# Three parts of a tuned transformer kernel: paired rounds of the value product, one plain weight slice instead of two, output weights prepared earlier

## The chip, the core and the metric

The kernel runs on one core of a Trainium2 chip as a single launch. The metric is the device time of one execution in microseconds. A core has five engines that run their own instruction streams and wait for each other with semaphores: TensorE (PE, matrix products and transposes), VectorE (DVE), ScalarE (ACT), GpSimd (POOL) and SyncE (SP, which issues DMAs). Weight loads of TensorE are shown as an engine of their own, PEld.

## The reference, cut to what matters

1024 tokens of width 512 pass six layers in float32. Two of them are a mixture of experts, one is a causal attention; these are the ones that the change touches.

```
x = x + 0.5 * ffn(layernorm(x))            # mixture of experts ("moe")
x = x + attn(layernorm(x))                 # causal attention ("causal")
x = x + 0.5 * ffn(layernorm(x))            # the same mixture of experts
x = x + 0.5 * butterfly(...); x = x + full_attention(...); x = x + 0.5 * butterfly(...)

# ffn: 16 experts, each token goes to 4 of them, and one shared expert
scores = sigmoid(x @ gate_w.T) + bias;  topk_w, topk_idx = top_k(scores, 4)
out = sum over chosen e of cw[e] * (silu(x @ Wg[e].T) * (x @ Wu[e].T)) @ Wd[e].T

# attn: 32 query heads of 16, 8 key/value heads, rotary embedding, causal mask
scores = einsum('bqhd,bkhd->bhqk', q, k) / 16
probs = softmax(where(mask, scores, min))
ctx = einsum('bhqk,bkhd->bqhd', probs, v)
out = ctx @ w_dense.T + b_dense
```

## The kernel before, in words

Each layer is one or more blocks; in a block every engine has its own list of instructions, and all engines meet at its end. Semaphore counts set the order between the engines, the written order sets it on an engine: an instruction that waits holds everything behind it on its engine.

**Split products.** A float32 product is made in one of two ways. "Plain" feeds float32 operands to TensorE (two recorded matmuls for each product). "Split" cuts both operands into a high part in the float32r type (`hi`, a cast on ScalarE) and the rest (`lo`, a subtraction on VectorE), and sums three products: hi with hi, hi with lo, lo with hi (`product`, L191).

**Routed blocks** (`routed_blocks`, L730 to L838). Tokens are sorted by expert into 47 blocks of 128 token slots, in each of the two mixture layers. For block b the engines do this:

- GpSimd gathers the rows of block b+3 (L708) and scatters the results of block b-3 with an add (L715).
- TensorE makes the gate and up product of block b: four slices of 128 inputs, of which the first `PLAIN` = 2 are plain (L730) and the other `SPLIT` = 2 split (L735). Then it transposes the rows of block b+2 (L744) and the hidden values of block b-1 (L751), and makes the down product of block b-2, split (L191).
- ScalarE casts the gate/up weights of block b+1 (L778, 1024 elements a partition), the down weights of block b+1 (L783), copies the output of block b-3 (L790), applies silu to block b (L795), casts the transposed rows of b+2 (L801) and the hidden values of b-1 (L806).
- VectorE makes the low parts of both weights (L819, L822), z = silu times up times routing weight (L828), a copy of the plain part of the transposed rows (L833), the low part of the split slices (L834), and the low part of the hidden values (L838).

ScalarE and VectorE read two table entries (expert and weight offset) into registers at the start of each step; w_hi and w_lo have two buffers each.

**Causal layer, core block** (L1469 on). The work goes in 8 groups of 4 query heads. A group has 12 steps u: u = 0 to 3 are query half 0 with key blocks 0 to 3; u = 4 to 11 are query half 1, where u = 4, 6, 8, 10 take key blocks 0 to 3 and u = 5, 7, 9, 11 key blocks 4 to 7. The steps on the diagonal are 0 to 3 and 5, 7, 9, 11. Step u has for each of 4 heads h a score product on TensorE (L1652, 128 to 512 columns), and an exponential on ScalarE (L1746) into the probability buffer `prob`. On a diagonal step GpSimd then zeroes a triangle of it (L1592, "mask"). When the step is complete, a round of values follows: V(u) is 4 plain products (one head each, 8 recorded matmuls) with `v_now`, each on 32 of the array's columns (L1669). TensorE issues V(u-1) in step u behind the third head. There are two `prob` buffers, so the exponentials of step u wait for V(u-2).

In between TensorE makes, for the next group, 48 products for row maxima (L1631, and L1634 on the diagonal), four in each step, which VectorE reduces (L1782); three PSUM banks hold the scores and three the maxima. GpSimd splits the maxima (L1558 to L1572; first half after mask 3, second half ahead of the next group), TensorE transposes them (L1642), ScalarE copies them after the exponentials of step 6 (L1731), and GpSimd then issues three small DMAs with them (`put_maxima`, L1578). On GpSimd's list this stands behind mask 5 and ahead of mask 7. In the last group nothing is made for a next one.

**Causal layer, dense block** (L1845 on). After the core block SP loads the output weights and the bias, ScalarE casts the weights to their high part (L1874, behind the casts of two tiles), GpSimd makes the low part (L1851) and adds the bias to all of x (L1853). TensorE transposes the 8 tiles of the context (L170), then makes 8 products of 12 matmuls (L191). VectorE makes the low parts (L182), waits for the bias, and adds each product to x (L1885), followed by its statistics (L86).

## Time and profile before

| | |
|---|---|
| time, median of 3 runs | 1372.45 us (1371.72 to 1373.23) |
| the profiled execution, its own time | 1367.37 us |
| its span, first to last instruction | 1365.6 us |
| PE busy | 1144.0 us (84%) |
| PEld busy | 723.2 us (53%) |
| DVE busy | 837.1 us (61%) |
| ACT busy | 665.5 us (49%) |
| POOL busy | 537.6 us (39%) |

The stages in order of time: mixture of experts to about 340 us (its 47 routed blocks from 85 us), causal layer from there to 766 us (its core block from 430 to 724 us, its dense block from 725 us), second mixture to about 1110 us, then butterfly, full attention and butterfly. Busy shares are averages over these stages. Instructions of register loads and semaphores are not counted as busy, so a gap whose cause is given as "issue" can be such work of the engine's own instruction reader.

### The profile page before, as it was taken

Reading aid. Unit: us, or ns where it says so; the run is one execution under the profiler, and the core shown is the slowest. Engines: PE = TensorE matmul, PEld = TensorE weight load, DVE = VectorE, ACT = ScalarE, POOL = GpSimd, SP = SyncE. Lnnn points to the kernel's source line nnn. Section 1 sums busy time; section 2 is a strip of 40 time slices with the busy share of each in tenths; the row PEclk is TensorE's granted clock in tenths of the full one; section 3 lists DMA queues with packets and bytes.
Section 4 is the critical chain, followed back from the end, with each engine's and each line's share of the span. In section 5 each row is a group of like instructions: output and inputs, shape, how many; then the busy total and the mean of one; then the engine's idle time right before and its main releaser. Section 6 shows DMA issues by size and latency. Waiting matters only on the chain. (4 is left out here: it accounts for less than half of the span.)

```text
span 1365.6 us, 22222 instructions
## 1 busy us (share of the span) xinstructions
PE 1144.0 (84%) x5800; PEld 723.2 (53%) x5801; DVE 837.1 (61%) x1527; ACT 665.5 (49%) x1218; POOL 537.6 (39%) x578
## 2 busy tenths in 40 slices
PE   5979999996284899999985796999999808777687
PEld 4747677674173344444424584676776605465454
DVE  4857777773455787777722565777777524445542
ACT  3136666663232277777772222666666503334133
POOL 4325555553673233333324324455555442050130
PEclk9979999998587699999998797999999957979879
DMA  9256989555405440000001454689955550010001
GB/s 349 100 203 156 241 238 248 100 104 90 183 35 133 95 89 2 1 1 1 1 1 39 181 189 170 179 206 264 253 107 100 81 167 0 4 37 0 20 12 62
DMA packets 63497, 151.64 MB, mean 111 GB/s; under 512 B 12560, under 2 KB 17488, under 8 KB 58832
## 3 DMA queue, kind: packets, MB, share of 16 engines
q1 hardware_dynamic: 40224, 99.83, 21.4%
q0 software_dynamic: 22592, 50.27, 19.4%
q10 hardware_dynamic: 624, 0.85, 0.4%
q8 instruction: 27, 0.44, 0.1%
q14 instruction: 30, 0.25, 0.1%
HBM read 105.75 MB, written 44.97 MB: 110 GB/s over the span
## 5 line engine op out<-in xcount | busy, mean ns | idle before, releaser
L715 POOL DMA_INDIRECT moe_acc_rows<-moe_out_rows,moe_token_of x94 | 165.4, 1760 | 196.5 <-ACT moe_out_rows L790 190.4
L1782 DVE TENSOR_REDUCE causal_top<-causal_mx 128x1 f32<-128x512 f32 (+3 forms) x384 | 192.0, 550 | 58.6 <-PE causal_mx L1634 50.5
L1746 ACT ACTIVATE causal_prob<-causal_sc 128x512 f32<-128x512 f32 (+3 forms) x384 | 169.9, 492 | 73.2 <-PE causal_sc L1652 70.7
L819 DVE TENSOR_TENSOR moe_w_lo<-moe_raw,moe_w_hi 128x1024 fp32r<-128x1024 f32 x94 | 115.1, 1225 | 112.7 <-ACT moe_w_hi L778 99.6
L730 PE MATMUL moe_gu<-moe_raw,moe_xt_plain 128*128 x376 | 180.5, 603 | 2.4 <-ACT moe_w_hi L778 2.4
L1631 PE MATMUL causal_mx<-causal_ks,causal_qs 96*128 (+4 forms) x384 | 130.9, 351 | 19.2 <-DMA causal_qs<-causal_parts 15.7
L778 ACT CAST moe_w_hi<-moe_raw 128x1024 fp32r x94 | 98.2, 1045 | 95.2 <-issue 90.8
L1652 PE MATMUL causal_sc<-causal_qs,causal_ks 99*128 (+3 forms) x384 | 123.7, 333 | 2.3 <-ACT causal_prob L1746 1.7
L708 POOL DMA_INDIRECT moe_rows<-moe_xn_rows,moe_token_of x94 | 93.3, 992 | 75.2 <-DVE moe_z L828 31.8
L822 DVE TENSOR_TENSOR moe_down_lo<-moe_raw,moe_down_hi 128x1024 fp32r<-128x1024 f32 x94 | 114.5, 1218 | 0.0
L735 PE MATMUL moe_gu<-moe_w_hi,xt_hi 128*128 128x512 f32 x188 | 112.7, 600 | 0.0
L730 PEld LDWEIGHTS moe_gu<-moe_raw,moe_xt_plain 128*128 128x128 f32 x376 | 71.6, 192 | 57.1 <-issue 49.4
L783 ACT CAST moe_down_hi<-moe_raw 128x1024 fp32r x94 | 98.1, 1043 | 0.0
L1592 POOL TENSOR_SCALAR_AFFINE_SELECT causal_prob<-causal_prob 128x512 f32<-128x512 f32 x64 | 40.9, 640 | 136.9 <-ACT causal_prob L1746 136.8
L1669 PE MATMUL causal_po<-causal_prob,causal_v_now 128*32 128x512 f32 (+3 forms) x768 | 81.8, 498 | 5.4 <-POOL causal_prob L1592 4.5
L1652 PEld LDWEIGHTS causal_sc<-causal_qs,causal_ks 99*128 (+1 forms) x384 | 36.8, 98 | 86.0 <-ACT causal_prob L1746 35.2
L191 PE MATMUL moe_y<-moe_down_hi,moe_zt_hi 128*128 128x512 f32 x188 | 81.9, 436 | 0.0
L735 PE MATMUL moe_gu<-moe_w_hi,xt_lo 128*128 128x512 f32 x188 | 74.5, 396 | 0.0
L191 PE MATMUL moe_y<-moe_down_hi,moe_zt_lo 128*128 128x512 f32 x188 | 74.2, 395 | 0.0
L735 PE MATMUL moe_gu<-moe_w_lo,xt_hi 128*128 128x512 f32 x188 | 74.1, 394 | 0.0
L191 PE MATMUL moe_y<-moe_down_lo,moe_zt_hi 128*128 128x512 f32 x188 | 73.9, 393 | 0.0
L145 POOL TENSOR_SCALAR var_eps<-mean_var 128x1 f32<-128x1 f32 x48 | 13.3, 276 | 147.6 <-DVE mean_var L98 147.4
(273 smaller groups left out, 2425.0 us busy)
## 6 DMA issues: line engine op xcount, KB each, us to landing
moe_raw<-in_w_gu SPq DMA_DIRECT2D x34, 1024.0 KB
moe_raw<-in_w_down SPq DMA_DIRECT2D x34, 512.0 KB
causal_qs<-causal_parts SPq DMA_DIRECT2D x42, 128.0 KB, 3.3
moe_acc_rows<-moe_zeros SPq DMA_DIRECT2D x2, 2304.0 KB, 15.2
moe_acc_rows<-x SPq DMA_DIRECT2D x18, 256.0 KB, 2.0
moe_xn_rows<-xn SPq DMA_DIRECT2D x2, 2048.0 KB, 10.9
x<-moe_acc_rows SPq DMA_DIRECT2D x16, 256.0 KB, 5.3
xn<-moe_acc_rows SPq DMA_DIRECT2D x16, 256.0 KB, 5.9
```

The lines of the kernel that those rows point to most:

```text
L191: last = nc.tensor.matmul(out, a, b, start=(n == 0), stop=(n == 3 * len(pairs) - 1))
L715: pool.indirect_dma_start(acc_rows[a], bass.IndirectOffsetOnAxis(ap=token_of[:, b - 3:b - 2].bitcast(U32), axis=0), out_rows[(b - 3) % OUT ...
L730: nc.tensor.matmul(gu[s][:, :], xt_plain[s][:, k, :], raw[:, bass.ds(at + k * 2 * FI, 2 * FI)], start=(k == 0), stop=False)
L735: last = nc.tensor.matmul(gu[s][:, :], xt(half, s, k), part[s][:, k - PLAIN, :], start=False, stop=(k == KT - 1 and half is m.xt_lo))
L778: nc.scalar.copy(w_hi[1 - s][:, :, :], raw[:, bass.ds(at + SPLIT_AT, GU_COLS - SPLIT_AT)].rearrange("p (k n) -> p k n", k=SPLIT)).then_inc ...
L783: nc.scalar.copy(down_hi[(c + 1) % 4][:, :, :], raw[:, bass.ds(at + GU_COLS, W_COLS - GU_COLS)].rearrange("p (i h) -> p i h", i=IT)).then_ ...
L819: nc.vector.tensor_tensor(w_lo[1 - s][:, :, :], raw[:, bass.ds(at + SPLIT_AT, GU_COLS - SPLIT_AT)].rearrange("p (k n) -> p k n", k=SPLIT), ...
L822: nc.vector.tensor_tensor(down_lo[(c + 1) % 4][:, :, :], raw[:, bass.ds(at + GU_COLS, W_COLS - GU_COLS)].rearrange("p (i h) -> p i h", i=I ...
L1631: last = nc.tensor.matmul(mx[i % BANKS][:, 0:w], qs[0:STACK, bass.ds(at, P)], ks[0:STACK, bass.ds(gn * S + kc * CH, w)], start=True, stop= ...
L1652: nc.tensor.matmul(sc[b][:, o:CH], ks[0:STACK + MROWS, bass.ds(g * S + kb * P, P)], qs[0:STACK + MROWS, bass.ds(g * QG + (h * S + c * CH + ...
L1746: nc.scalar.activation(prob[u % 2][:, h, o:CH], sc[(u * QPK + h) % BANKS][:, o:CH], ACT.Exp, scale=SCALE).then_inc(exp_done, 1)
L1782: nc.vector.tensor_reduce(top[:, kc, t, h:h + 1], mx[i % BANKS][:, 0:w], AX.X, ALU.max).then_inc(mx_read, 1)
```

## The change

`PLAIN` becomes 1, so three of four gate/up slices are split; the buffers of the output rows move into `m.xn`. In the core block the rounds of values are issued in pairs, V(u-2) and V(u-1) behind the third head of each even step u, and `prob` has three buffers, so that the exponentials of step u wait for V(u-3). The output weights are loaded in the core block in two halves; GpSimd casts, subtracts and adds the bias there, one slice and one tile a group, in `prepare_dense`, which stands in step 6 behind `put_maxima`. The dense block keeps the transposes, the products and the additions, with the transposes of the next tile ahead of each product, and VectorE finishing tile t-2 behind the low part of tile t.

```diff
--- before.py
+++ after.py
@@ -34,7 +34,7 @@
 EARLY = 3
-PLAIN = 2
+PLAIN = 1
 SPLIT = KT - PLAIN
@@ -625,7 +625,7 @@
         rows = [sb(f"rows{s}", [P, ROW]) for s in range(RING)]
-        out_rows = [sb(f"out_rows{s}", [P, H]) for s in range(OUTS)]
+        out_rows = [m.xn[:, s, :] for s in range(OUTS)]
         xt_plain = [sb(f"xt_plain{s}", [P, PLAIN, P]) for s in range(2)]
@@ -1273,6 +1273,7 @@
         ks = outer.enter_context(nc.sbuf_tensor(f"{name}_ks", [P, KV * S], BF16))
+        dense_in, wd_half, wd_ready, x_biased = sem("dense_in"), sem("wd_half"), sem("wd_ready"), sem("x_biased")
@@ -1478,6 +1479,8 @@
+            wd_hi = outer.enter_context(nc.sbuf_tensor(f"{name}_wd_hi", [P, KT, H], F32R))
+            wd_lo = outer.enter_context(nc.sbuf_tensor(f"{name}_wd_lo", [P, KT, H], F32R))
             BANKS = 3
@@ -1486,6 +1489,8 @@
             ident = sb("ident", [P, P], BF16)
+            wd_raw = sb("wd_raw", [P, KT // 2, H])
+            b_out = sb("b_out", [P, H])
             warm = sb("warm", [1, 1])
@@ -1493,7 +1498,8 @@
             neg_turned = [sb(f"neg_turned{h}", [MROWS * QPK, CH], BF16) for h in range(NCH)]
-            prob = [sb(f"prob{s}", [P, QPK, CH]) for s in range(2)]
+            PROBS = 3
+            prob = [sb(f"prob{s}", [P, QPK, CH]) for s in range(PROBS)]
             out_t = sb("out_t", [P, CH])
@@ -1539,9 +1545,13 @@
                         sp.dma_start(ks[a * HD:(a + 1) * HD, 0:S], parts_dram[K_PART[a], 0:HD, :]).then_inc(stack_in, 16)
+                    sp.dma_start(wd_raw[:, :, :], m.dram["w_dense"][:, 0:KT // 2, :]).then_inc(dense_in, 16)
+                    sp.dma_start(b_out[:, :], m.dram["b_dense"].rearrange("(a h) -> a h", a=1).broadcast_to([P, H])).then_inc(dense_in, 16)
                     with sp.Fori(1, KV) as g:
...
                         load(g)
+                    sp.wait_ge(wd_ready, KT // 2)
+                    sp.dma_start(wd_raw[:, :, :], m.dram["w_dense"][:, KT // 2:KT, :]).then_inc(dense_in, 16)
@@ -1589,8 +1599,22 @@
                         pool.wait_ge(exp_done, g * (NS * QPK) + ((u + 1) * QPK + BANKS))
-                        nc.gpsimd.affine_select(prob[u % 2][:, :, o:o + P], prob[u % 2][:, :, o:o + P], [[0, QPK], [1, P]],
+                        nc.gpsimd.affine_select(prob[u % PROBS][:, :, o:o + P], prob[u % PROBS][:, :, o:o + P], [[0, QPK], [1, P]],
                                                 ALU.is_ge, 0.0, base=0, channel_multiplier=-1).then_inc(masked, 1)
+                    def prepare_dense(g):
+                        if g == 0:
+                            pool.wait_ge(dense_in, 32)
+                        if g == KT // 2:
+                            pool.wait_ge(dense_in, 48)
+                        if g < KT:
+                            raw = wd_raw[:, g % (KT // 2), :]
+                            nc.gpsimd.tensor_copy(wd_hi[:, g, :], raw).then_inc(wd_half, 1)
+                            pool.wait_ge(wd_half, g + 1)
+                            nc.gpsimd.tensor_tensor(wd_lo[:, g, :], raw, wd_hi[:, g, :].bitcast(F32),
+                                                    ALU.subtract).then_inc(wd_ready, 1)
+                        nc.gpsimd.tensor_tensor(m.x[:, g, :], m.x[:, g, :], b_out[:, :], ALU.add).then_inc(x_biased, 1)
@@ -1605,6 +1629,8 @@
                                 put_maxima(g + 1, 0)
+                            if u == C0 + 2:
+                                prepare_dense(g)
@@ -1667,7 +1693,7 @@
                             last = nc.tensor.matmul(po[2 * HD * h:2 * HD * (h + 1), o:CH], v_now[:, kb, :],
-                                                    prob[u % 2][:, h, o:CH], start=(kb == 0), stop=(kb == (c + 1) * TC - 1))
+                                                    prob[u % PROBS][:, h, o:CH], start=(kb == 0), stop=(kb == (c + 1) * TC - 1))
                         last.then_inc(pv_done, 1)
@@ -1685,9 +1711,11 @@
                                     maximum(g + 1, UPS * u + h)
-                                if h == 2 and u >= 1:
+                                if h == 2 and u % 2 == 0 and u >= 2:
+                                    values(g, u - 2)
                                     values(g, u - 1)
-                                elif h == 2 and not first:
+                                elif h == 2 and u == 0 and not first:
+                                    values(g - 1, NS - 2)
                                     values(g - 1, NS - 1)
@@ -1718,6 +1746,7 @@
                     group(KV - 1, False, False)
+                    values(KV - 1, NS - 2)
                     values(KV - 1, NS - 1)
@@ -1739,11 +1768,11 @@
                             o = max(0, kb * P - c * CH)
-                            if some(g * NS + u):
-                                act.wait_ge(pv_done, g * NS + u)
+                            if some(g * NS + u - 1):
+                                act.wait_ge(pv_done, g * NS + u - 1)
                             for h in range(QPK):
                                 act.wait_ge(sc_done, g * (NS * QPK) + (u * QPK + h + 1))
-                                nc.scalar.activation(prob[u % 2][:, h, o:CH], sc[(u * QPK + h) % BANKS][:, o:CH], ACT.Exp,
+                                nc.scalar.activation(prob[u % PROBS][:, h, o:CH], sc[(u * QPK + h) % BANKS][:, o:CH], ACT.Exp,
                                                      scale=SCALE).then_inc(exp_done, 1)
@@ -1829,62 +1858,45 @@
-            wd_raw = sb("wd_raw", [P, KT, H])
-            wd_hi = sb("wd_hi", [P, KT, H], F32R)
-            wd_lo = sb("wd_lo", [P, KT, H], F32R)
-            b_out = sb("b_out", [P, H])
             xp = [pb(f"xpd{s}", [P, CH]) for s in range(2)]
...
             cm = NormSems(sem, "ctx")
-            wd_in, wd_half, wd_ready, x_biased, y_done, x_done = (
-                sem("wd_in"), sem("wd_half"), sem("wd_ready"), sem("x_biased"), sem("y_done"), sem("x_done"))
+            y_done, x_done = sem("y_done"), sem("x_done")
             with nc.Block() as block:
-                @block.sync
-                def _(sp):
-                    sp.dma_start(wd_raw[:, :, :], m.dram["w_dense"]).then_inc(wd_in, 16)
-                    sp.dma_start(b_out[:, :], m.dram["b_dense"].rearrange("(a h) -> a h", a=1).broadcast_to([P, H])).then_inc(wd_in, 16)
-                @block.gpsimd
-                def _(pool):
-                    pool.wait_ge(wd_half, 1)
-                    nc.gpsimd.tensor_tensor(wd_lo[:, :, :], wd_raw[:, :, :], wd_hi[:, :, :].bitcast(F32),
-                                            ALU.subtract).then_inc(wd_ready, 1)
-                    nc.gpsimd.tensor_tensor(m.x[:, :, :], m.x[:, :, :], b_out[:, :].unsqueeze(1).broadcast_to([P, T, H]),
-                                            ALU.add).then_inc(x_biased, 1)
                 @block.tensor
                 def _(pe):
-                    for t in range(T):
-                        transpose_tile(m, pe, cm, xp[t % 2], t, ready=False)
-                    pe.wait_ge(wd_ready, 1)
-                    for t in range(T):
-                        pe.wait_ge(cm.xt_lo, t + 1)
-                        if t >= 2:
-                            pe.wait_ge(x_done, t - 1)
-                        rows = slice(t * P, (t + 1) * P)
-                        product(nc, yp[t % 2][:, :], [(m.xt_hi[:, k, rows], m.xt_lo[:, k, rows], wd_hi[:, k, :], wd_lo[:, k, :])
-                                                      for k in range(KT)]).then_inc(y_done, 1)
+                    pe.wait_ge(wd_ready, KT)
+                    for t in range(T + 1):
+                        if t < T:
+                            transpose_tile(m, pe, cm, xp[t % 2], t, ready=False)
+                        if t >= 1:
+                            pe.wait_ge(cm.xt_lo, t)
+                            if t >= 3:
+                                pe.wait_ge(x_done, t - 2)
+                            rows = slice((t - 1) * P, t * P)
+                            product(nc, yp[(t - 1) % 2][:, :], [(m.xt_hi[:, k, rows], m.xt_lo[:, k, rows], wd_hi[:, k, :],
+                                                                 wd_lo[:, k, :]) for k in range(KT)]).then_inc(y_done, 1)
...
                 def _(act):
-                    for t in range(2):
-                        hi_tile(m, act, cm, xp[t % 2], t)
-                    act.wait_ge(wd_in, 32)
-                    nc.scalar.copy(wd_hi[:, :, :], wd_raw[:, :, :]).then_inc(wd_half, 1)
-                    for t in range(2, T):
+                    for t in range(T):
                         hi_tile(m, act, cm, xp[t % 2], t)
...
                 def _(dve):
-                    for t in range(T):
-                        lo_tile(m, dve, cm, xp[t % 2], t)
-                    dve.wait_ge(x_biased, 1)
-                    for t in range(T):
+                    def finish(t):
                         dve.wait_ge(y_done, t + 1)
...
+                    dve.wait_ge(x_biased, T)
+                    for t in range(T):
+                        lo_tile(m, dve, cm, xp[t % 2], t)
+                        if t >= 2:
+                            finish(t - 2)
+                    finish(T - 2)
+                    finish(T - 1)
```

## Rows read from the trace of the kernel before

**Rows 1.** Busy time by stretch: stretch, length, busy (instructions) by engine, clock, DMA share, GB/s.

```profile
480.00:720.00 240.00, 230.37 (x1723) 92.89 (x1715) 168.49 (x351) 170.40 (x390) 76.71 (x173) 1.00 0.06 13
```

**Rows 2.** Timeline, TensorE, one routed block: start us, us, engine, line, operation, count.

```profile
203.96 1.88 PE L730 MATMUL moe_gu<-moe_raw,moe_xt_plain 128*128 x4
...
205.91 0.40 PE L735 MATMUL moe_gu<-moe_w_lo,xt_hi 128*128 128x512 f32 x1
...
207.07 0.60 PE L744 MATMUL moe_tx<-ident,moe_rows 128*128 128x128 f32 x4
...
209.12 1.88 PE L730 MATMUL moe_gu<-moe_raw,moe_xt_plain 128*128 x4
```

**Rows 3.** Groups by line and form: count | busy us, mean ns | idle before, releaser.

```profile
L819 DVE TENSOR_TENSOR moe_w_lo<-moe_raw,moe_w_hi 128x1024 fp32r<-128x1024 f32 x94 | 115.1, 1225 | 112.7 <-ACT moe_w_hi L778 99.6 <-issue 13.0
...
L778 ACT CAST moe_w_hi<-moe_raw 128x1024 fp32r x94 | 98.2, 1045 | 95.2 <-issue 90.8 <-SPq L676 4.5
```

**Rows 4.** Timeline, routed blocks, ScalarE: hidden values, weights of the next, silu.

```profile
202.81 0.38 ACT L806 CAST moe_zt_hi<-moe_tz 128x256 fp32r<-128x256 f32 x1
...
204.19 1.05 ACT L778 CAST moe_w_hi<-moe_raw 128x1024 fp32r x1 [1.00 <-issue]
...
207.27 0.39 ACT L795 ACTIVATE moe_silu<-moe_gu 128x256 f32<-128x256 f32 x1 [0.61 <-PE moe_gu L735]
```

**Rows 5.** Timeline, routed blocks, VectorE: an early step, and the end of a later one.

```profile
98.42 1.22 DVE L819 TENSOR_TENSOR moe_w_lo<-moe_raw,moe_w_hi 128x1024 fp32r<-128x1024 f32 x1
...
102.18 1.23 DVE L819 TENSOR_TENSOR moe_w_lo<-moe_raw,moe_w_hi 128x1024 fp32r<-128x1024 f32 x1
...
224.30 0.41 DVE L838 TENSOR_TENSOR moe_zt_lo<-moe_tz,moe_zt_hi 128x256 fp32r<-128x256 f32 x1
225.99 1.23 DVE L819 TENSOR_TENSOR moe_w_lo<-moe_raw,moe_w_hi 128x1024 fp32r<-128x1024 f32 x1 [1.27 <-issue]
```

**Rows 6.** Timeline, core block, GpSimd: the same instruction in two groups that follow.

```profile
597.16 0.40 POOL L1584 COPY causal_v_now<-causal_v_all 128x256 f32<-128x256 f32 x1
...
629.51 0.40 POOL L1584 COPY causal_v_now<-causal_v_all 128x256 f32<-128x256 f32 x1
```

**Rows 7.** Timeline, core block, TensorE: a wait, and a round of values with its neighbours.

```profile
607.14 0.23 PE L1631 MATMUL causal_mx<-causal_ks,causal_qs 96*128 x1 [0.20 <-DVE causal_top L1782]
...
608.33 0.38 PE L1631 MATMUL causal_mx<-causal_ks,causal_qs 96*128 x1
608.63 1.07 PE L1669 MATMUL causal_po<-causal_prob,causal_v_now 128*32 128x512 f32 x8
609.63 0.39 PE L1652 MATMUL causal_sc<-causal_qs,causal_ks 99*128 x1
```

**Rows 8.** Timeline, core block: end of step 6 on ScalarE, then GpSimd's put and mask 7.

```profile
613.17 0.60 ACT L1746 ACTIVATE causal_prob<-causal_sc 128x512 f32<-128x512 f32 x1 [0.79 <-PE causal_sc L1652]
...
614.52 1.62 POOL L1578 DMA_DIRECT2D causal_qs<-causal_neg_turned  x3 [3.15 <-ACT causal_neg_turned L1731]
616.38 0.64 POOL L1592 TENSOR_SCALAR_AFFINE_SELECT causal_prob<-causal_prob 128x512 f32<-128x512 f32 x1 [0.23 <-ACT causal_prob L1746]
```

**Rows 9.** Groups by line and form on GpSimd, columns as in rows 3.

```profile
L133 POOL TENSOR_TENSOR x<-x,xn 128x512 f32<-128x512 f32 x16 | 20.1, 1259 | 23.2 <-POOLq L620 23.2
...
L914 POOL CAST butter_perm_row<-butter_perm_row_i 128x512 f32<-128x512 int32 x2 | 1.7, 843 | 0.0
L1099 POOL TENSOR_TENSOR full_wo_lo<-full_wo_raw,full_wo_hi 128x512 fp32r<-128x512 f32 x1 | 1.4, 1443 | 0.0
```

**Rows 10.** Timeline, dense block: first transposes, first addition, last matmul.

```profile
725.35 1.94 PE L170 MATMUL causal_xpd<-ident,xn 128*128 128x128 f32 x8 [1.93 <-PEq L1527]
...
747.02 0.69 DVE L1885 TENSOR_TENSOR x<-causal_yp,x 128x512 f32<-128x512 f32 x1 [6.48 <-POOL x L1853]
...
764.44 0.40 PE L191 MATMUL causal_yp<-causal_wd_hi,xt_lo 128*128 128x512 f32 x1
```

**Rows 11.** Start of the core block: the stretch of its first loads, columns as in rows 1.

```profile
432.00:434.00 2.00, 0.00 (x0) 0.00 (x0) 0.08 (x1) 0.95 (x1) 0.00 (x0) 0.50 1.11 147
```

4 lines of the change are left out of this document (2 added, 2 removed).

## The prediction, made before the changed kernel was run

> **What bounds the kernel now.** I read the page's busy shares first (TensorE 84%, the next engine 61%), then the busy time by stretch, then the timelines of one routed block, one group of the core block and the dense block, because an average over six stages prices nothing. The reader is to see three things. In the core block TensorE is busy 230.37 of 240 us [rows 1]. In a routed block it has no gap at all: one block follows the other after 209.12 - 203.96 = 5.16 us [rows 2], and 94 blocks make 485 us of the span. In the dense block the order is set by preparation: the first addition waits for GpSimd's bias until 747.02, while TensorE had started at 725.35 [rows 10]. So TensorE's time counts in two stages, and waiting in the third.
>
> **One plain slice instead of two.** The matmuls of one kind follow each other at (207.07 - 205.91) / 5 = 0.232 us, so the first split one ran at 205.68 and two plain slices took 205.68 - 203.96 = 1.72 us, 0.86 each [rows 2]. A split slice is three matmuls, 0.70 us. Each block saves 0.16 us of TensorE, 94 blocks 15.0 us, and the period becomes 5.00.
>
> What pays is elsewhere. The weight cast grows from 1024 to 1536 elements: at most in proportion, 0.52 us on 1.045 (ScalarE) and 0.61 us on 1.225 (VectorE) [rows 3]; the cast of the transposed rows grows by half as well, some 0.13 us at the same rate, and VectorE's copy loses what its subtraction gains. ScalarE has 0.61 us to spare before silu [rows 4], and needs up to 0.65 more in a period 0.16 shorter. It is short by up to 0.20 on this count. Against that stands its gap of 1.00 us marked "issue" ahead of the weight cast [rows 4]: the register loads of a step stand behind the cast of the hidden values, which waits for TensorE. An engine that is late finds that wait already met and loads while it still computes; VectorE did so in the early step, 98.42 to 102.18, 3.76 us with no gap [rows 5]. I take it that ScalarE does the same and hides the shortage. VectorE needs 3.76 + 0.61 = 4.37 us of 5.00. The first block of each layer has nothing to hide the longer cast and subtraction: +0.5 us twice. Sum -14.0; bounds -15.0 and, if ScalarE hides nothing, (5.20 - 5.16) x 94 = +3.8.
>
> **Rounds of values in pairs.** A round of 512 columns starts 0.30 us after the last matmul ahead of it, of which 0.23 is that matmul's own stream, and the next score product starts 1.00 us later [rows 7]: 1.07 us, where the same columns cost 0.86 in a plain slice. So a round pays 0.21 us to get in and out, and a pair pays once, if its second round runs into the first. The Trainium skill, "TensorEngine Tiling (Array Packing)", section Key Properties, says that changing the tiling mode drains TensorE while tiles within a mode work independently. By that rule the whole 0.21 is saved in each pair, 10.1 us; the trace shows a cost of that form, but no two rounds side by side. The other bound is the 0.07 ahead of a round alone, 3.4 us. I take 0.20 x 48 pairs = 9.6 us, nearer to the rule's form because the four products of a round already overlap.
>
> TensorE also idles 9.6 us in 240 [rows 1], with a period of 629.51 - 597.16 = 32.35 us [rows 6] some 1.3 us a group; part are waits for VectorE's reductions [rows 7] and for masks. V(u-2) now stands ahead of V(u-1) and covers the mask's 0.64. On the other side the three PSUM banks run empty in a pair of 1.9 us, and ScalarE and VectorE restart from nothing after it. Between all idle gone (-1.3 x 7 = -9) and 0.25 us lost at each pair (+10) I take -4.5, the masks' part. Pairing: -14.1, bounds -19 and +7.
>
> **The dense preparation on GpSimd.** It stands behind `put_maxima` and ahead of mask 7, and that mask is what V(7) waits for; behind V(7) stand the fourth score of step 8 and all that follows on TensorE. The put starts at 614.52 and takes 1.62, to 616.14 [rows 8]. The prepared slice costs a cast of 0.84, a subtraction of 1.44 and the bias of 1.26 [rows 9], 3.54 us, then two hand-overs of 0.1 and the mask 0.64: mask 7 is done at about 620.5. TensorE wants it sooner. The step's last exponential ended at 616.38 - 0.23 = 616.15 [rows 8] with V(6) ahead of it on TensorE; V(6) now moves behind three more scores, ScalarE's own rate lets the exponential come some 0.45 earlier (615.7), V(6) then starts near 616.3 and V(7) could at 617.2. The stall is 3.3 us in groups 0 to 3. In groups 4 to 6 only the bias is added: 616.14 + 1.26 + 0.64 + 0.1 = 618.15, a stall of 0.95. Group 7 has no put. Sum 4 x 3.3 + 3 x 0.95 = +16.1; bounds +19 (both tensor operations at 1.44 and the cast at 1.26) and +8 (the pair comes 2 us later, because ScalarE restarts late). Before, this work lay behind the core block; nothing hides it here but GpSimd's idle time, and the place in its list is what takes that away.
>
> **The dense block.** It ended at 764.44 + 0.23 = 764.67 [rows 10]. Now weights and bias are ready. Two tiles are transposed in 1.94 us at the lower clock, 725.35 to 727.3; with the wait for the first low part the first product starts at 727.9 and, at twice 0.232 a matmul as long as the clock is low, ends at 733.5. Seven products of 12 x 0.232 = 2.79 and six transposed tiles of about 0.5 (four transposes recorded 0.60, rows 2) give 22.5: end 756.0, -8.7 us. Bounds -5 (the low clock lasts a product longer) and -10.5 (it rises at once).
>
> **Loads at the start of the core block.** 0.5 MB of weights and 0.25 MB of bias now stand on SP's queue behind the first key loads and beside the first query loads on ScalarE's. The DMA engines are full there, 1.11, at 147 GB/s [rows 11], so 0.77 MB cost 5.2 us if all ahead of the queries, nothing if all behind. I take half, +2.5. The second half of the weights waits on SP behind all group loads, where nobody needs SP. The output rows in `m.xn` add no instruction: 0.
>
> **Sum.** -14.0 - 14.1 + 16.1 - 8.7 + 2.5 = -18.2 us. The profiled execution took 1367.37 us around a span of 1365.6; it becomes 1349.2. The median of the runs is 5.1 us above it, and the same step from there gives 1372.45 - 18.2 = 1354 us.
>
> **Rivals.**
> 1. The mask is not late. For it: GpSimd is busy only 76.71 of 240 us [rows 1], and a pair may start later than I reckon. Against: the order of its list, and 3.5 us do not fit between the put and the mask. Then 1354 - 16 = 1338 us.
> 2. ScalarE bounds the routed blocks. For it: the shortage of up to 0.20 us. Against: its register loads can overlap once it is late. With growth in proportion the period is 5.20 and the time 1354 + 18 = 1372; with 0.1 less, 1362.
> 3. The pairs starve the other engines and pairing gives nothing: 1354 + 14 = 1368 us. For it: the three banks; against: VectorE waits for TensorE as often as the reverse.
> 4. The other side: VectorE's register loads don't overlap in the looped part. There they lie bare, 224.30 to 225.99, 1.69 us from the start of the last subtraction to the next weight subtraction, marked "issue" [rows 5]. If so its step is 3.76 + 0.61 + 1.69 - 0.41 = 5.65 us. It decides as soon as a step passes 5.16: 94 x (5.65 - 5.00) = +61, 1415 us. Against: the early steps made the same loads within 3.76 us, and the later gap stands where VectorE had time.
>
> **How the numbers follow.** The forecast 0.60, rival 1 0.12, rival 2 0.16, rival 3 0.05, rival 4 0.07. The forecast's own range is 1346 to 1362. The range of 1342 to 1368 takes in the bounds of the single terms and most of rival 2, and leaves out rivals 1 and 4 and a remainder, some 0.2. About 0.2%, 2.7 us, is what a measurement of this kernel can tell from no change. Faster by more: the forecast, rival 1, most of rivals 2 and 3, 0.87; within it 0.05, from rivals 2 and 3; slower 0.08, rival 4 and the worst of rival 2.
>
> **What would show it.** Right: routed blocks 5.00 us apart with no gap on TensorE; 8 + 8 value matmuls in 1.9 us; V(7) waiting for mask 7 some 3 us in groups 0 to 3, 1 us in groups 4 to 6; the dense block's last product near 31 us after its first transpose; the first maximum product of the core block 2 to 3 us later. Wrong: gaps on TensorE in the routed blocks ending with the weight subtraction; mask 7 ready before V(6) ends; a second round that costs 1.07 again; a group period of the core block far from 34 us in groups 0 to 3 and 31.5 us in groups 4 to 6.

## The result, and the profile after

The changed kernel takes 1380.51 us (median of 6 runs, 1375.74 to 1385.47), the kernel before 1370.59 beside it (6 runs): ratio 1.0074, 95% interval 1.0052 to 1.0096, so 7 to 13 us slower. Ratios below are against runs of the kernel before that were taken beside each kernel. The prediction said 1354. The profiled execution took 1379.36 us around a span of 1377.6.

The stages, each from its first instruction on TensorE to the first (or last) of the next, us:

```
stage                                               before   after  difference
start to the first routed block, layer 1             86.10   84.79   -1.3
routed blocks, layer 1                              243.86  242.35   -1.5
first transpose of the attention layer to scores    107.11  108.67   +1.6
core block, first score to last transpose           257.29  278.95  +21.7
dense block, first transpose to last product         39.49   30.15   -9.3
routed blocks, layer 2                              244.87  244.33   -0.5
all other                                           386.88  388.36   +1.5
```

These are one profiled execution each. The loss is in the core block, and the routed blocks give 2 us where 14 were forecast. The third stage holds the new loads: it takes 108.1 to 108.7 us in the four traces with them, and 105.8 to 107.1 in the eight traces of kernels that are as before up to there.

TensorE's share of busy time hardly moves, and would not tell where to look. This is the page's line, and then the stretch that [rows 1] shows of before: busy 218.33 of 240 us where it was 230.37.

```profile
PE 1136.6 (83%) x5894; PEld 743.7 (54%) x5895; DVE 879.0 (64%) x1527; ACT 708.5 (51%) x1217; POOL 589.4 (43%) x592
```

```profile
480.00:720.00 240.00, 218.33 (x1595) 93.11 (x1597) 164.83 (x345) 151.85 (x351) 88.67 (x181) 0.98 0.06 15
```

**Routed blocks.** An undisturbed block is as predicted: 208.63 - 203.64 = 4.99 us on TensorE (before 5.16, [rows 2]). But some blocks are not undisturbed. The second row below has TensorE waiting 1.05 us at the row transposes for the gather:

```profile
203.64 1.02 PE L730 MATMUL moe_gu<-moe_raw,moe_xt_plain 128*128 x2
...
208.63 1.02 PE L730 MATMUL moe_gu<-moe_raw,moe_xt_plain 128*128 x2
...
218.01 0.66 PE L744 MATMUL moe_tx<-ident,moe_rows 128*128 128x128 f32 x4 [1.05 <-DMA moe_rows<-moe_xn_rows,moe_token_of]
```

Such waits, past the start of each layer, are 10.6 us in 12 after and 0.8 us in one before. From one silu to the next, the 46 intervals of a layer sum to 232.3 and 234.2 us. Were the last 44 of each 4.98 us, they would sum to 226.7; before, they sum to 233.6 and 234.6. So the shorter block could give 15 us and gives under 2: 13 are lost in the stretched ones, some 10 of them in these waits, which are all in the first 30 blocks of a layer, while weights are still being loaded.

The casts and subtractions grew less than in proportion (1475 and 1760 ns, [rows 3] had 1045 and 1225, columns as there):

```profile
L819 DVE TENSOR_TENSOR moe_w_lo<-moe_raw,moe_w_hi 128x1536 fp32r<-128x1536 f32 x94 | 165.4, 1760 | 74.9 <-ACT moe_w_hi L778 74.8
```

```profile
L778 ACT CAST moe_w_hi<-moe_raw 128x1536 fp32r x94 | 138.7, 1475 | 83.2 <-issue 79.2 <-SPq L676 4.0
```

GpSimd's timeline says why the gather is late. First after, then before; L715 is the scatter of the output rows, L708 the gather of a later block:

```profile
202.58 2.29 POOL L715 DMA_INDIRECT moe_acc_rows<-xn,moe_token_of  x1 [1.42 <-ACT xn L790]
205.17 0.99 POOL L708 DMA_INDIRECT moe_rows<-moe_xn_rows,moe_token_of  x1 [0.30 <-issue]
```

```profile
202.29 1.75 POOL L715 DMA_INDIRECT moe_acc_rows<-moe_out_rows,moe_token_of  x1 [2.13 <-ACT moe_out_rows L790]
204.35 0.99 POOL L708 DMA_INDIRECT moe_rows<-moe_xn_rows,moe_token_of  x1 [0.30 <-issue]
```

After, the gather goes out 205.17 - 203.64 = 1.53 us behind its block's first matmul; before, 204.35 - 203.96 = 0.39 [rows 2]. Of the 1.14, 0.54 is the scatter itself. The rest is its later start: it waits for ScalarE's copy of the output rows, which stands behind the longer cast. The rows are wanted at the transposes of the next block, 7.9 us behind the gather before and 6.4 after (one block of each). The gathers of the changed kernel landed 3.9 to 4.4 us after their issue once all weights were there, and up to 8.4 us after it before that.

**Core block.** The group period was 32.35 [rows 6]. It is 614.64 - 577.07 = 37.57 in groups 1 to 3 and 34.10 in groups 4 to 6. Group 0 took 33.97, where it was 31.36 before:

```profile
577.07 0.40 POOL L1594 COPY causal_v_now<-causal_v_all 128x256 f32<-128x256 f32 x1 [0.17 <-PE causal_po L1695]
...
614.64 0.40 POOL L1594 COPY causal_v_now<-causal_v_all 128x256 f32<-128x256 f32 x1 [0.17 <-PE causal_po L1695]
...
648.74 0.40 POOL L1594 COPY causal_v_now<-causal_v_all 128x256 f32<-128x256 f32 x1 [0.17 <-PE causal_po L1695]
```

GpSimd in group 3: the put, the three prepared operations, then mask 7. Below it TensorE: a pair in one piece (16 recorded matmuls and 1.86 us to the next score), then V(6), and V(7), 2.41 us late for that mask.

```profile
595.65 1.61 POOL L1588 DMA_DIRECT2D causal_qs<-causal_neg_turned  x3 [3.62 <-ACT causal_neg_turned L1760]
597.26 0.63 POOL L1613 CAST causal_wd_hi<-causal_wd_raw 128x512 fp32r<-128x512 f32 x1
597.97 1.27 POOL L1615 TENSOR_TENSOR causal_wd_lo<-causal_wd_raw,causal_wd_hi 128x512 fp32r<-128x512 f32 x1
599.20 1.26 POOL L1617 TENSOR_TENSOR x<-x,causal_b_out 128x512 f32<-128x512 f32 x1
600.41 0.63 POOL L1602 TENSOR_SCALAR_AFFINE_SELECT causal_prob<-causal_prob 128x512 f32<-128x512 f32 x1
```

```profile
592.02 1.92 PE L1695 MATMUL causal_po<-causal_prob,causal_v_now 128*32 128x512 f32 x16
593.88 0.39 PE L1678 MATMUL causal_sc<-causal_qs,causal_ks 99*128 x1
...
597.63 1.06 PE L1695 MATMUL causal_po<-causal_prob,causal_v_now 128*32 128x512 f32 x8
601.10 1.30 PE L1695 MATMUL causal_po<-causal_prob,causal_v_now 128*32 128x384 f32 x8 [2.41 <-POOL causal_prob L1602]
602.33 0.61 PE L1678 MATMUL causal_sc<-causal_qs,causal_ks 99*128 x1
```

The price goes on behind the wait: that score product takes 0.61 us where others take 0.39. TensorE had idled for 2.41 us, and the clock granted behind it is 0.54 of full speed, its level of 1.2 GHz for most of the stretch:

```profile
596.00:598.60 2.60, 2.60 (x18) 0.95 (x17) 2.59 (x5) 2.28 (x6) 2.52 (x5) 1.00 0.03 5
601.10:604.40 3.30, 3.30 (x17) 1.64 (x18) 0.56 (x1) 0.60 (x1) 0.00 (x0) 0.54 0.00 0
```

The clock doesn't fall each time. In group 0 TensorE waits 2.46 us for the same mask, the granted clock of the group stays 1.00, and against the pairs alone (below) the group loses 2.6 us instead of 4.2.

**Dense block.** First transpose, first product, last matmul: 776.48 - 746.73 = 29.75 us, 39.09 in [rows 10]; no wait for GpSimd is left in it.

```profile
746.73 1.06 PE L170 MATMUL causal_xpd<-ident,xn 128*128 128x128 f32 x8 [2.39 <-PEq L1533]
748.82 0.80 PE L191 MATMUL causal_yp<-causal_wd_hi,xt_hi 128*128 128x512 f32 x1 [1.03 <-DVE xt_lo L182]
...
776.48 0.40 PE L191 MATMUL causal_yp<-causal_wd_hi,xt_lo 128*128 128x512 f32 x1
```

### The profile page after: what moved, and what is told of

Its sections match the earlier page's. It is cut to its first block and busy times, and to the rows that moved or that the text cites. A ratio compares the mean times of both kernels' runs of the same rounds, so it can differ in the third digit from the quotient of the medians.

```text
span 1377.6 us, 22328 instructions
## 1 busy us (share of the span) xinstructions
PE 1136.6 (83%) x5894; PEld 743.7 (54%) x5895; DVE 879.0 (64%) x1527; ACT 708.5 (51%) x1217; POOL 589.4 (43%) x592
## 5 line engine op out<-in xcount | busy, mean ns | idle before, releaser
L715 POOL DMA_INDIRECT moe_acc_rows<-xn,moe_token_of x94 | 210.1, 2236 | 144.7 <-ACT xn L790 135.8
L819 DVE TENSOR_TENSOR moe_w_lo<-moe_raw,moe_w_hi 128x1536 fp32r<-128x1536 f32 x94 | 165.4, 1760 | 74.9 <-ACT moe_w_hi L778 74.8
L778 ACT CAST moe_w_hi<-moe_raw 128x1536 fp32r x94 | 138.7, 1475 | 83.2 <-issue 79.2
L735 PE MATMUL moe_gu<-moe_w_hi,xt_hi 128*128 128x512 f32 x282 | 147.8, 524 | 0.6 <-DVE moe_w_lo L819 0.6
L708 POOL DMA_INDIRECT moe_rows<-moe_xn_rows,moe_token_of x94 | 95.8, 1019 | 77.0 <-DVE moe_z L828 35.2
L822 DVE TENSOR_TENSOR moe_down_lo<-moe_raw,moe_down_hi 128x1024 fp32r<-128x1024 f32 x94 | 114.5, 1218 | 0.0
L735 PE MATMUL moe_gu<-moe_w_hi,xt_lo 128*128 128x512 f32 x282 | 112.4, 399 | 0.0
L735 PE MATMUL moe_gu<-moe_w_lo,xt_hi 128*128 128x512 f32 x282 | 112.1, 397 | 0.0
L730 PE MATMUL moe_gu<-moe_raw,moe_xt_plain 128*128 x188 | 98.0, 603 | 3.2 <-ACT moe_w_hi L778 3.2
L1695 PE MATMUL causal_po<-causal_prob,causal_v_now 128*32 128x512 f32 (+3 forms) x768 | 76.4, 509 | 11.3 <-POOL causal_prob L1602 11.3
L744 PE MATMUL moe_tx<-ident,moe_rows 128*128 128x128 f32 x376 | 59.1, 281 | 23.7 <-DMA moe_rows<-moe_xn_rows,moe_token_of 23.5
L1678 PEld LDWEIGHTS causal_sc<-causal_qs,causal_ks 99*128 (+1 forms) x384 | 37.3, 98 | 71.1 <-issue 36.8
L1657 PEld LDWEIGHTS causal_mx<-causal_ks,causal_qs 96*128 (+1 forms) x384 | 38.3, 100 | 66.2 <-issue 30.8
```

Source lines behind the costliest of these rows:

```text
L715: pool.indirect_dma_start(acc_rows[a], bass.IndirectOffsetOnAxis(ap=token_of[:, b - 3:b - 2].bitcast(U32), axis=0), out_rows[(b - 3) % OUT ...
L730: nc.tensor.matmul(gu[s][:, :], xt_plain[s][:, k, :], raw[:, bass.ds(at + k * 2 * FI, 2 * FI)], start=(k == 0), stop=False)
L735: last = nc.tensor.matmul(gu[s][:, :], xt(half, s, k), part[s][:, k - PLAIN, :], start=False, stop=(k == KT - 1 and half is m.xt_lo))
L778: nc.scalar.copy(w_hi[1 - s][:, :, :], raw[:, bass.ds(at + SPLIT_AT, GU_COLS - SPLIT_AT)].rearrange("p (k n) -> p k n", k=SPLIT)).then_inc ...
L819: nc.vector.tensor_tensor(w_lo[1 - s][:, :, :], raw[:, bass.ds(at + SPLIT_AT, GU_COLS - SPLIT_AT)].rearrange("p (k n) -> p k n", k=SPLIT), ...
L822: nc.vector.tensor_tensor(down_lo[(c + 1) % 4][:, :, :], raw[:, bass.ds(at + GU_COLS, W_COLS - GU_COLS)].rearrange("p (i h) -> p i h", i=I ...
```

## The experiments

### Each part alone

**The pairs alone.** The kernel before with this and three probability buffers:

```diff
-                                if h == 2 and u >= 1:
+                                if h == 2 and u % 2 == 0 and u >= 2:
+                                    values(g, u - 2)
                                     values(g, u - 1)
```

> The kernel before with the pairs of value rounds and three probability buffers, and nothing else of the change. Theory (the pairs starve the other engines through the three score banks and the three maximum banks): the second round of a pair saves its 0.2 us, but the group period of the core block rises from 32.35 to 33.3 to 33.7 us, 8 groups +8 to +11, about 1380 us against 1371; ScalarE's waits for the score products in the core block grow by more than 15 us in all. Rival (the pairing does what was predicted and the whole loss of the core block belongs to the preparation on GpSimd): a period near 30.6 us and about 1357 us.

Measured: 1373.21 us against 1369.32, ratio 1.0024 (1.0011 to 1.0037), a loss of 1.5 to 5 us, and a group period of 633.69 - 600.33 = 33.36. In the stretch from 470 to 720 us the rounds are cheaper and no longer wait for masks (3.4 us before), but the score products wait 8.3 us for ScalarE where they waited 1.7. The groups of the pair kernel in that stretch, then of the kernel before:

```profile
L1653 PE MATMUL causal_sc<-causal_qs,causal_ks 99*128 (+4 forms) x365 | 118.0, 331 | 10.3 <-ACT causal_prob L1750 8.3 <-issue 1.3
...
L1670 PE MATMUL causal_po<-causal_prob,causal_v_now 128*32 128x512 f32 (+3 forms) x736 | 70.6, 502 | 0.0
```

```profile
L1652 PE MATMUL causal_sc<-causal_qs,causal_ks 99*128 (+4 forms) x378 | 120.2, 329 | 2.3 <-ACT causal_prob L1746 1.7 <-DMA causal_qs<-causal_neg_turned 0.3
...
L1669 PE MATMUL causal_po<-causal_prob,causal_v_now 128*32 128x512 f32 (+3 forms) x760 | 81.4, 500 | 4.3 <-POOL causal_prob L1592 3.4 <-ACT causal_out_t L1736 0.2
```

The period is as the theory had it; the time, at +3.3 us, is under its +8 to +11: the last group, which has no maxima to make, is 1.6 us shorter with pairs (29.2 to 27.6). ScalarE's waits for score products in the core block grew by 7.4 us (70.7 to 78.1), not by the 15 expected. The rival, the prediction's own -14, is out.

The saved mask waits lie in that last group. These are a whole group and the last group of the kernel before:

```profile
597.16:629.51 32.35, 31.74 (x242) 13.24 (x240) 25.36 (x53) 22.83 (x54) 10.84 (x27) 1.00 0.00 1
694.20:723.40 29.20, 22.17 (x154) 7.07 (x154) 1.37 (x4) 20.05 (x49) 7.09 (x13) 0.98 0.01 2
```

In the whole group TensorE idles 0.61 us, of which 0.10 is a wait for a mask; in the last group its waits for masks are 4.3 us, and 0.1 with pairs, while its waits for ScalarE at the scores grow from 1.7 to 3.6. ScalarE's timeline there shows seven exponentials in one run, (3.56 - 0.60) / 6 = 0.49 us apart:

```profile
612.52 3.56 ACT L1750 ACTIVATE causal_prob<-causal_sc 128x512 f32<-128x512 f32 x7
```

**One plain slice alone.** The kernel before with `PLAIN = 1` and the output rows in `m.xn`.

> The kernel before with one plain slice instead of two in the routed blocks, output rows in m.xn, and nothing else. Theory (gathers come late): undisturbed blocks 4.98 us apart, but TensorE waits at the row transposes for the gather some 50 to 55 us in all against 28 before, and the time falls by only 2 to 4 us, to about 1368. Rival (the loss came from elsewhere in the changed kernel): waits at the row transposes as before, 28 us, and 1357 us.

Measured: 1370.75 us, ratio 1.0006 (0.9987 to 1.0025): nothing, of the 14 us predicted. TensorE's waits for gathers at the transposes are 23.7 us in all (12.9 before, the start of each layer included):

```profile
L744 PE MATMUL moe_tx<-ident,moe_rows 128*128 128x128 f32 x376 | 59.6, 282 | 23.9 <-DMA moe_rows<-moe_xn_rows,moe_token_of 23.7
```

The 28 us and 50 to 55 us of the expectation were sums over the matmuls and the weight loads of the transposes, which wait side by side; by the matmuls alone it is 12.9 before, 23.5 in the changed kernel and 23.7 here. The verdict is the theory's.

**The preparation and the dense block.** The changed kernel with the other two parts taken back.

> The kernel before with the preparation of the dense weights on GpSimd in step 6 of a group and the new dense block, with single value rounds, two probability buffers and two plain slices. Theory (both parts of the core block's loss are real and independent): V(7) waits for its mask in groups 0 to 3 by some 3 us and in groups 4 to 6 by under 1, core block +12, dense block -9, start of the core block +1.6: about 1375 us. Rival (the preparation is harmless without the pairs): -9 + 1.6, about 1364 us. Rival (the preparation is the whole loss of the core block, +21.7): about 1385 us.

Measured: 1380.46 us, ratio 1.0088 (1.0068 to 1.0109), +9 to +15, between the theory and the second rival. The core block takes 277.2 us (+19.9), with a period of 35.1 to 36.8 us in groups 0 to 3 and 33.2 in 4 to 6; the dense block 29.3 (-10.2). So the preparation costs 19.9 us where the theory had 12: 4.2 us in the mean of groups 0 to 3 and 0.9 in 4 to 6. What the clock costs can be read here, from groups 2 and 3. TensorE waits 2.71 us for mask 7 in both; the clock stays up in the first and falls in the second, and the group is 1.64 us longer:

```profile
543.44:578.58 35.14, 31.85 (x242) 13.23 (x240) 25.39 (x53) 22.83 (x54) 13.91 (x30) 1.00 0.00 1
578.58:615.36 36.78, 33.46 (x242) 14.01 (x240) 25.52 (x53) 22.92 (x53) 13.90 (x29) 0.95 0.00 1
```

The three parts alone sum to +16 where the whole change costs +10; the four intervals together allow a difference of some 5, so how far the parts hide each other isn't settled.

**The preparation in another place.** One line of the changed kernel:

```diff
-                            if u == C0 + 2:
+                            if u == C0 + 5:
                                 prepare_dense(g)
```

> The changed kernel with the preparation of the dense weights behind mask 9 instead of behind the put of the maxima, so that no value round of that pair of steps waits for it; all else as in the changed kernel. Theory: the stall of 2.5 us and the low clock behind it go in groups 0 to 3 and 0.6 us in groups 4 to 6: group period about 34 us in groups 0 to 3 too, 12 to 14 us off the changed kernel's 1380.5, about 1367. Rival (GpSimd's reads slow VectorE's reductions wherever they stand, and the place is not what matters): less than 4 us off, 1377 or more.

Measured: 1363.16 us, against before 0.9950 (0.9932 to 0.9968), 17 under the changed kernel, more than the 12 to 14 expected: the same instructions, three steps later in GpSimd's list. The period is 632.74 - 599.37 = 33.37, within 0.3 us that of the pairs alone in groups 1 to 6 (the theory had about 34), and 32.0 in group 0 (31.3 with the pairs alone); below, a later group, with the bias behind mask 9. The place was the whole cost; the rival (GpSimd slowing VectorE) is out.

```profile
599.37 0.40 POOL L1594 COPY causal_v_now<-causal_v_all 128x256 f32<-128x256 f32 x1 [0.17 <-PE causal_po L1695]
...
624.22 0.64 POOL L1602 TENSOR_SCALAR_AFFINE_SELECT causal_prob<-causal_prob 128x512 f32<-128x512 f32 x1 [4.00 <-ACT causal_prob L1775]
624.82 1.27 POOL L1617 TENSOR_TENSOR x<-x,causal_b_out 128x512 f32<-128x512 f32 x1
...
632.74 0.40 POOL L1594 COPY causal_v_now<-causal_v_all 128x256 f32<-128x256 f32 x1 [0.17 <-PE causal_po L1695]
```

### Why the gathers are late

**Gather ahead of scatter.** One plain slice, and GpSimd's list turned round: the scatter of block b-3 follows the next gather instead of going ahead of it (the waits and buffers of the scatter moved with it).

```diff
-            for b in range(-3, NB + 3):
+            for b in range(-3, NB + 4):
 ...
-                if there(b - 3):
-                    a = (b - 3) % 2
+                if there(b - 4):
+                    a = (b - 4) % 2
```

> As the kernel with one plain slice alone, but GpSimd issues the gather for a block ahead of the scatter that stood before it in its list (each scatter is one gather later). Theory (the gather is late because the longer scatter, 2.24 us against 1.76, stands ahead of it): the gather goes out some 0.4 us after the block's first matmul instead of 1.5, TensorE's waits for it at the row transposes fall from 24 us to about 13 (the kernel before has 13), and the time is 10 us under the one-slice kernel's 1370.8, about 1360. Rival (the gathers are late because their transfers share the DMA engines with the weight loads in a shorter period, whenever they are issued): waits stay at 20 us or more and the time at 1367 or more.

Measured: 1358.15 us, ratio 0.9927 (0.9907 to 0.9947), 11 us under one slice alone by the two ratios. The gather goes out 200.15 - 199.72 = 0.43 us behind the block's first matmul, and TensorE's waits for gathers are 15.4 us (23.7).

```profile
L744 PE MATMUL moe_tx<-ident,moe_rows 128*128 128x128 f32 x376 | 58.8, 280 | 15.4 <-DMA moe_rows<-moe_xn_rows,moe_token_of 15.4
```

```profile
200.15 0.98 POOL L708 DMA_INDIRECT moe_rows<-moe_xn_rows,moe_token_of  x1 [2.11 <-DVE moe_z L828]
```

So the order of one list decided it, with the same transfers and weight loads; gathers still landed up to 9.1 us after their issue. The rival is out, but for the 2.5 us of waits by which this kernel stays above the one before.

**What made the scatter longer.** Two kernels with one half each: the output rows in `m.xn` with two plain slices, and one plain slice with output rows of their own.

> The kernel before with the output rows of the routed blocks in m.xn, two plain slices. Theory (the scatter is longer in the changed kernel because the longer casts move it under VectorE's subtraction of the down weights): a mean of 1.76 us, as before. Rival (its new source makes it longer): 2.2 us.

> The kernel before with one plain slice, its output rows in buffers of their own as before. Theory (overlap with VectorE's subtraction): a mean scatter of 2.24 us and TensorE's waits for gathers near 20 to 24 us. Rival (the new source in m.xn): 1.76 us and waits near 13.

One run each, 1366.58 and 1369.34 us, too few for a verdict on the time; TensorE's waits for gathers are 13.4 and 26.0 us. The scatter's group, first and second kernel:

```profile
L715 POOL DMA_INDIRECT moe_acc_rows<-xn,moe_token_of x94 | 165.5, 1760 | 196.7 <-ACT xn L790 190.3
```

```profile
L715 POOL DMA_INDIRECT moe_acc_rows<-moe_out_rows,moe_token_of x94 | 209.9, 2233 | 148.0 <-ACT moe_out_rows L790 141.3
```

The place is innocent. What counts is whether VectorE is in the middle of a weight subtraction (L819, L822) when the scatter starts. This one of the changed kernel ends at 203.41, 0.83 us into the scatter of 202.58, which took 2.29:

```profile
202.19 1.22 DVE L822 TENSOR_TENSOR moe_down_lo<-moe_raw,moe_down_hi 128x1024 fp32r<-128x1024 f32 x1
```

In the kernel before, 85 of the 94 scatters start in such a subtraction, with 0.28 to 0.80 us of it left, and each takes that rest and 1.43 to 1.52 us more; the other nine take 1.55 to 1.59. In the changed kernel 84 start in one, and the same holds for 82 of them; the other two take 1.2 us more still. The mean rest is 0.29 us before and 0.74 after, nearly all of the 0.47 by which the mean scatter grew. It isn't the overlap as such. In the kernel with the gather ahead, a scatter that starts 0.10 us ahead of a subtraction and runs beside it takes 1.59 us; one that starts 0.13 us behind another takes 3.09, its rest of 1.63 and 1.46 more:

```profile
126.87 1.59 POOL L715 DMA_INDIRECT moe_acc_rows<-xn,moe_token_of  x1 [0.30 <-issue]
131.81 3.09 POOL L715 DMA_INDIRECT moe_acc_rows<-xn,moe_token_of  x1 [0.30 <-issue]
```

```profile
126.97 1.76 DVE L819 TENSOR_TENSOR moe_w_lo<-moe_raw,moe_w_hi 128x1536 fp32r<-128x1536 f32 x1 [0.66 <-ACT moe_w_hi L778]
131.68 1.76 DVE L819 TENSOR_TENSOR moe_w_lo<-moe_raw,moe_w_hi 128x1536 fp32r<-128x1536 f32 x1 [0.44 <-ACT moe_w_hi L778]
```

The Trainium skill, "SBUF — State Buffer", section SBUF: two separate sides, has the pair of ports that VectorE and GpSimd share as an exclusive lock, where the loser waits and doesn't share, and says of a VectorE operation with two SBUF inputs that it locks only against GpSimd operations that read SBUF. The scatter's wait for the rest agrees; the operation that waited here is an indirect DMA, whose row numbers (`token_of`) lie in SBUF. The subtraction that started behind a scatter took its 1.76 us all the same, so no run here shows VectorE held back for the whole of a scatter.

### Why the pairs gain nothing

**Other banks.** The pairs, and single rounds as their control, with four score banks and two for the maxima instead of three and three:

> The kernel before with pairs of value rounds and three probability buffers, and four score banks and two maximum banks instead of three and three. Theory (in pairs TensorE waits for the exponentials because three score banks hold too little): the waits of the score products for ScalarE, 8.3 us over the groups with three banks, fall under 3 us, and the group period from 33.37 to about 32.6 us; against single rounds with the same banks it is no more than 0.3 us longer. Rival (ScalarE's rate of one exponential in 0.49 us against 0.44 us for a score and a maximum product bounds the stretch between two pairs, whatever the banks): waits stay, period 33.2 or more.

> The kernel before (single value rounds, two probability buffers) with four score banks and two maximum banks: the control for the pairs with these banks. Theory: the score products' waits, 2.3 us, go, and the maximum products wait more for VectorE with two banks; group period 32.3 to 32.8 us against 32.35, 1369 to 1373 us.

Measured: 1418.33 us (1.0365, 1.0341 to 1.0389) and 1418.73 (1.0372, 1.0347 to 1.0397), periods 37.5 to 40.0 and 38.4. Neither theory had that. With two maximum banks the maximum products wait for VectorE's reductions 26.4 and 29.3 us in the stretch, and that hides what four score banks do:

```profile
L1633 PE MATMUL causal_mx<-causal_ks,causal_qs 96*128 (+4 forms) x307 | 102.7, 337 | 29.0 <-DVE causal_top L1787 26.4
```

As a test of the score banks it is inconclusive. It shows how much the third maximum bank is worth here.

**Short exponentials.** Pairs, and single rounds, with the exponentials over half of their columns (the other half of `prob` stays at one, so both kernels compute something else):

```diff
-  prob[...][:, h, o:CH], sc[...][:, o:CH], ACT.Exp
+  prob[...][:, h, o:(o + CH) // 2], sc[...][:, o:(o + CH) // 2], ACT.Exp
```

> The kernel before with pairs of value rounds, three probability buffers, and exponentials of the left half of each tile's columns only (the other half of the probabilities stays at one, so the values are not the reference's). Theory (a pair pays on TensorE what was predicted, 0.2 us and the mask's waits, but ScalarE, at 0.49 us an exponential, can't feed the scores between two pairs): with short exponentials the waits of the score products, 8.3 us over the groups, fall under 2 us and the group period is 30.5 to 31.3 us, at least 0.8 us under the single rounds' with the same exponentials. Rival (the pairs lose on TensorE itself or on VectorE's maxima): the period stays at 32.3 us or more and not below the single rounds'.

> The kernel before with single value rounds, two probability buffers and exponentials of the left half of each tile's columns only: the control for the pairs with short exponentials. ScalarE hardly bounds single rounds (their score products wait 2.3 us in all), so both theories expect a group period of 31.9 to 32.3 us against 32.35.

Measured: pairs 1362.15 us (0.9929, 0.9896 to 0.9962), period 627.13 - 594.87 = 32.26; single 1368.24 (0.9971, 0.9954 to 0.9989), period 32.24. The pairs' waits for ScalarE fall to 1.9 us as the theory had it, and pairs gain 1.1 us a group by it where single rounds gain 0.1. So what the pairs lose against before is ScalarE's. But the period stops at 32.26, not at 30.5 to 31.3: something else takes over. Most of the 6 us between the two times lies in the last group, which makes no maxima: 23.1 us with pairs, 28.4 with single rounds. There, with ScalarE's work halved, pairs do pay.

```profile
L1653 PE MATMUL causal_sc<-causal_qs,causal_ks 99*128 (+4 forms) x373 | 117.8, 329 | 4.9 <-ACT causal_prob L1750 1.9 <-issue 1.3 <-DMA causal_qs<-causal_neg_turned 0.8
```

**Short exponentials and short maxima.** The same two, and the reductions over half of the columns too (`mx[...][:, 0:w // 2]`); the scale of the exponentials is a thousandth as large.

> The kernel before with pairs of value rounds and three probability buffers, exponentials of the left half of each tile's columns at a scale a thousandth as large, and maxima over the left half of each product's columns (so the values are not the reference's). Theory (what short exponentials left of the loss is VectorE's rate between two pairs, 0.54 to 0.59 us a reduction): group period 30.4 to 31.0 us, 1.2 to 1.8 under the single rounds with the same short work. Rival (the pairs lose it on TensorE): period not below 32.0, level with the single rounds.

> The kernel before with single value rounds, two probability buffers, and the same short exponentials and short maxima: the control. TensorE waits little for VectorE in single rounds (2.0 us in all at the maximum products), so both theories expect 31.7 to 32.2 us a group.

Measured: pairs 1344.12 us (0.9798, 0.9753 to 0.9843), single 1350.65 (0.9851, 0.9808 to 0.9895). GpSimd's copy in two groups that follow, pairs and then single:

```profile
584.00 0.40 POOL L1585 COPY causal_v_now<-causal_v_all 128x256 f32<-128x256 f32 x1 [0.92 <-PE causal_po L1670]
614.54 0.40 POOL L1585 COPY causal_v_now<-causal_v_all 128x256 f32<-128x256 f32 x1 [0.92 <-PE causal_po L1670]
```

```profile
586.33 0.40 POOL L1584 COPY causal_v_now<-causal_v_all 128x256 f32<-128x256 f32 x1
617.01 0.40 POOL L1584 COPY causal_v_now<-causal_v_all 128x256 f32<-128x256 f32 x1
```

30.54 and 30.68 us. The pairs' period is as forecast, but the control's was expected at 31.7 to 32.2 and fell by as much: VectorE's reductions cost single rounds 1.56 us a group too, though TensorE's maximum products of the kernel before show only 2.0 us of waits for them in the whole stretch. The theory that only the pairs pay VectorE has fallen. Pairs gain 0.14 us a group, not 1.2 to 1.8. In one group of each, the rounds are 0.85 us shorter in sum (8.81 against 9.66, each to the next matmul), and the scores and maximum products between them take 0.7 us longer (20.3 against 19.7). What holds these stays open. The last group is again shorter with pairs, 24.4 against 27.4, and some 6 us of both kernels' gain stand ahead of the first score, where the first group's maxima are made.

### A version from what was found

Single rounds, the preparation behind mask 9, the gather ahead of the scatter, and the rest of the change.

> The changed kernel with single value rounds, the preparation of the dense weights behind mask 9, and the gather ahead of the scatter in GpSimd's list. Theory: routed blocks -10 to -14, core block as before (group period 32.4), dense block -9, start of the core block +1.6: 1347 to 1352 us. Rival (the late gathers can't be mended by the order of the list): 1358 to 1362.

Measured: 1349.71 us against 1369.66, ratio 0.9860 (0.9836 to 0.9883): 20 us faster than the kernel before, inside the 1347 to 1352 expected, and about 30 faster than the changed one. Group period 32.35, core block 256.9 us as before, dense block 29.8.

## Why the prediction was wrong

- **One plain slice (-14.0; measured alone +0.8, interval -1.8 to +3.4).** The period of 5.00 was right (4.99), and so was that ScalarE hides its shortage: rivals 2 and 4 did not come. The step that failed is the one that priced only TensorE, ScalarE and VectorE and took GpSimd's list as given ("what pays is elsewhere" stopped at two engines). The scatter stood ahead of the gather in it, grew by 0.47 us in the mean and began later, and the gather had a slack of 6.4 us instead of 7.9, less than some transfers took beside the weight loads (up to 8.4). "The output rows in `m.xn` add no instruction: 0" was right.
- **Pairs (-14.1; measured +3.3, interval +1.5 to +5.1).** The drain (-9.6) was sized well: two rounds of 512 columns take 1.86 us to the next score where two single ones take 2.00, and the 0.07 ahead of a round is paid once. Two steps failed. The first is "-4.5, the masks' part": it spread the 9.6 idle us of [rows 1] over seven groups, 1.3 us each, but a whole group has 0.61, of which 0.10 is a mask's, and the waits for masks lie in the last group. The second is the bound on the other side. "The three PSUM banks run empty" was named, priced at up to +0.25 a pair, and then outweighed by that idle time. Between two pairs eight scores come without a break, and ScalarE's exponentials follow 0.49 us apart where a score and a maximum product take 0.44; the group became 1.0 us longer. Rival 3 was the right mechanism, at 0.05, and its worst case (nothing gained) was still too kind.
- **The reading behind both.** The prediction took TensorE's 230.37 busy us of 240 for the bound of the core block. In a whole group it is 31.74 in 32.35; with short exponentials and maxima the same matmuls ran in 30.68, less than had been "busy". Part of the recorded busy time was waiting. The Trainium skill, "Perfetto Trace Analysis", section Identifying the Most-Contended Engine, says that a matmul busy share is no good measure of distance from the roofline because matmuls are pipelined. That it misleads agrees with these two periods; here it showed too much work, not too little.
- **Preparation (+16.1).** Right in place and cause: 17 us by moving it alone, 19.9 by adding it without pairs. That the size came out is partly luck. The stall was 2.41 us instead of 3.3: GpSimd's three operations took 3.15 us with no hand-overs between them, so the mask was done 0.5 us sooner than reckoned (the cast took 0.63, not the 0.84 of [rows 9], which is a cast from int32), and V(7) could start 0.4 later. The slow matmuls behind the stall, which the sum had left out, made it good. Against the pairs alone, by group: (33.97 - 31.34) + (37.57 - 33.37) x 3 + (34.10 - 33.37) x 3 = 17.
- **Dense block (-8.7), loads (+2.5).** Measured -9.3 and +1.6.

The sum: -18.2 forecast, +10 measured; 28 us apart. By the kernels with one part each, the slice is 15 of it and the pairs 17; the preparation with dense block and loads took 2 more than forecast, and together that is some 6 more than the 28, the part that isn't settled above. The chances gave slower 0.08, all of it in cases about VectorE's registers and ScalarE; neither of the two causes stood there.

## What to carry to other kernels

When a block becomes shorter, walk every engine's list around it, the one that only issues DMAs above all: what stands ahead of the transfer that is needed next, and how much slack it had. Work put on an idle engine costs what stands behind it in that engine's list; three steps later it cost nothing. Batching the bound engine's work helps only if its feeders keep up between the batches, and a busy share of 96% says little about that: shorten the feeders' work once and see whether the period moves. And read idle time for a loop from one turn of the loop: a stretch that takes in its last, different turn puts that turn's waits on all the others.

## What was not expected of the hardware

- GpSimd's indirect scatter took 1.55 to 1.59 us when VectorE was in no subtraction of two SBUF operands at its start, and 1.43 to 1.52 us plus the rest of the subtraction when it was (85 of 94 scatters before); a subtraction that began 0.10 us later added nothing.
- TensorE's recorded busy time held waits: 31.74 us a group, where the same matmuls fit into 30.68.
- A wait of 2.41 us on TensorE was followed by 3.3 us at a mean granted clock of 0.54, and the group took 4.2 us more than one without it (37.57 against 33.37). Waits of 2.46 and 2.71 us in other groups were not followed by a fall; in the kernel with the preparation alone the fall cost 1.64 us.
- One maximum bank less, 3 to 2, and one score bank more: 49 us, 38.47 us a group instead of 32.35.
